# Highs and lows of four heads one above the other in one operand of the spread products

## The reference, cut to what matters

```python
xn  = layernorm(x)                                     # x: 32 batches x 512 tokens x 256
q   = heads(xn @ Wq + bq); k = heads(xn @ Wk + bk)     # 16 heads of 16 columns
val = heads(xn @ Wv + bv)
pos = heads(sinusoid @ Wp + bp)
content   = einsum('bhsp,bhtp->bhst', q + u, k)
pos_score = relative_shift(einsum('bhsp,htp->bhst', q + v, pos))
weights   = softmax((content + pos_score) / 4)
att = (weights @ val) @ Wo + bo
out = x + att + routed_ffn(xn)                         # 8 experts, top 128 of 512 tokens, gelu
```

## Time and profile before

| | us |
|---|---|
| median of 3 runs | 5023.73 |
| lowest, highest | 5016.13, 5023.78 |
| the profiled execution | 5030.14 |
| its span in the trace | 5028.3 |

### The profile page before, as it was taken

How to read it: one execution, slowest core, us unless ns; L and a number is a source line. 1 busy time by engine, 2 the same in 40 slices (tenths; PEclk the granted TensorE clock), 3 DMA queues, 4 the chain that set the end, 5 groups by cost and what they waited for, 6 DMA issues and landing times. The chain is left out here.

```text
span 5028.3 us, 126515 instructions
## 1 busy us (share of the span) xinstructions
PE 4825.9 (96%) x42412; PEld 3683.7 (73%) x42412; DVE 3691.6 (73%) x8040; ACT 3462.9 (69%) x5180; POOL 1711.7 (34%) x1545
## 2 busy tenths in 40 slices
PE   7899999999999999999999999989999999999997
PEld 3566666676676666766666667758999898998997
DVE  7799998898898888988888889874455545444344
ACT  3688888898888888988978889864433333344454
POOL 1122222232223222322222222224566565544443
PEclk9899999999999999999999999999999999999999
DMA  9899999999999999999999999986445455433359
GB/s 351 318 361 347 332 360 342 351 361 337 366 349 345 362 335 346 366 343 359 359 328 360 339 344 366 366 296 179 100 115 141 113 133 140 109 62 68 60 146 312
DMA packets 320461, 1391.16 MB, mean 277 GB/s; under 512 B 42912, under 2 KB 120608, under 8 KB 188448
## 3 DMA queue, kind: packets, MB, share of 16 engines
q1 hardware_dynamic: 196896, 778.35, 41.7%
q0 software_dynamic: 122880, 604.05, 39.3%
HBM read 708.00 MB, written 674.23 MB: 275 GB/s over the span
## 5 line engine op out<-in xcount | busy, mean ns | idle before, releaser
L745 DVE CUSTOM_DVE_ANT_0 att_shifted<-att_quad,att_shifted 128x512 f32<-128x512 f32 x2048 | 1327.1, 684 | 213.2 <-PE att_quad L990 170.5
L610 ACT ACTIVATE att_shifted<-att_shifted,att_mn 128x512 f32<-128x512 f32 x2048 | 1361.9, 717 | 122.0 <-issue 100.4
L605 ACT ACTIVATE ring<-att_quad 128x1024 f32<-128x1024 f32 x1024 | 1047.1, 1023 | 310.8 <-PE att_quad L978 309.5
L1011 PE MATMUL att_tp<-ident,att_shifted 128*128 128x128 f32 x8192 | 1134.4, 282 | 7.1 <-issue 4.4
L755 DVE COPY att_pt<-att_tp 128x512 f32<-128x512 f32 x1536 | 1011.8, 686 | 141.2 <-PE att_tp L1011 124.0
L1011 PEld LDWEIGHTS att_tp<-ident,att_shifted 128*128 128x128 f32 x8192 | 886.8, 142 | 308.3 <-issue 145.4
L497 POOL DMA_DIRECT2D att_shifted<-xs_d x512 | 279.3, 545 | 2249.7 <-DMA xs_d<-ring 1259.3
L1482 DVE TENSOR_TENSOR ffn_hp<-ring,ffn_hp 128x512 fp32r<-128x512 f32 x512 | 474.6, 927 | 683.8 <-ACT ring L1419 638.3
L1417 ACT ACTIVATE ffn_hp<-ffn_up 128x512 fp32r<-128x512 f32 x512 | 306.0, 598 | 920.5 <-PE ffn_up L1563 864.8
L978 PE MATMUL att_quad<-att_pos,att_qv 64*128 64x512 f32 x2048 | 848.1, 454 | 38.3 <-ACT ring L605 38.2
L990 PE MATMUL att_quad<-att_kd,att_qu 64*128 64x512 f32 x2048 | 787.0, 456 | 68.9 <-issue 50.0
(11 more groups left out here) (111 smaller groups left out, 4707.7 us busy)
## 6 DMA issues: line engine op xcount, KB each, us to landing
xs_d<-ring SPq DMA_DIRECT2D x512, 1026.0 KB, 9.4
att_shifted<-xs_d POOLq DMA_DIRECT2D x512, 1024.0 KB, 9.9
att_shifted<-in_L_attn_x_dram SPq DMA_DIRECT2D x32, 512.0 KB, 7.2
xn_d<-att_shifted SPq DMA_DIRECT2D x32, 512.0 KB, 6.5
xt_d<-att_shifted SPq DMA_DIRECT2D x32, 512.0 KB, 7.6
gathered<-xt_d SPq DMA_DIRECT2D x32, 512.0 KB, 11.6
att_d<-att_osb SPq DMA_DIRECT2D x512, 32.0 KB
ring<-in_L_ffn_w_dram SPq DMA_DIRECT2D x16, 1024.0 KB
```

The source lines that it names most:

```text
L605: act.activation(xo[:, kk % NW, 2 * half:2 * half + 2, 1:S + 1], xp[:, :, :], ACT.Copy).then_inc(x_out, 1)
L610: act.activation(shifted[:, kk % NX, t], shifted[:, kk % NX, t], ACT.Exp, bias=mn[:, kk % NX, t:t + 1], scale=-1.0).then_inc(exp_done, 1)
L745: dve.tensor_tensor_reduce(out=shifted[:, kk % NX, t], in0=sp_[:, t % 2], in1=shifted[:, kk % NX, t], scale=-0.25, scalar=-NEG, op0=ALU.ad ...
L1011: ins = pe.transpose(tp[:, c % 2, t * P:(t + 1) * P], shifted[:, kk % NX, t, c * P:(c + 1) * P], ident[:, :])
```

## The change

Four heads (64 rows) are taken at a time. The high parts of four heads stand in one half of the partitions and their low parts in the other half of the same operand, so that `spread_out` is one product where it was two. `qc[:, k, 0]` held the highs of a tile's eight heads and `qc[:, k, 1]` their lows. Now index 0 holds the highs of the first four heads (partitions 0 to 63, `FORMER`) above the lows of the same four (64 to 127, `LATER`), and index 1 the same of the last four. `kc` likewise.

For that POOL's split of a tile, a copy and a subtraction over 128 partitions, becomes four instructions, each behind the one before: the copy of all highs; the subtraction for the last four heads, within their half; the subtraction for the first four, which reads partitions 0 to 63 and writes 64 to 127; and a copy of the last four's highs, which reads 64 to 127 and writes 0 to 63. The last three have 64 partitions and the same 512 elements in each. The counts of the semaphores `high` become three a tile. At the start, ACT and DVE split the two tiles of positions in the same manner (one more instruction each a tile). The constant `spread` is loaded whole in one DMA, where a cleared tile and eight small loads were. The scores, softmax, values and the FFN phase are untouched.

```diff
     spread = np.zeros((P, 2, 2, P), np.float32)
-    for head in range(MH):
+    for head in range(QH):
         for kind in range(2):
             for copy in range(COPIES):
-                row = head % GH * ROWS + copy * HD
-                spread[head * HD:(head + 1) * HD, kind, 1 - picks_high[kind][copy], row:row + HD] = np.eye(HD)
+                column = head % GH * ROWS + copy * HD
+                row = head * HD if picks_high[kind][copy] else P // 2 + head * HD
+                spread[row:row + HD, kind, head // GH, column:column + HD] = np.eye(HD)
...
-                sp.wait_ge(spread_zero, 1)
-                for kind in range(2):
-                    for k in range(MH // GH):
-                        rows = slice(k * GH * HD, (k + 1) * GH * HD)
-                        at = spread_at[kind] + k * P
-                        sp.dma_start(spread[rows, at:at + P].bitcast(F32), spread_d[rows, kind, 0]).then_inc(const_in, 16)
+                sp.dma_start(spread[:, :, :, :].bitcast(F32), spread_d).then_inc(const_in, 16)
...
                     pool.tensor_copy(by_tile(qc[:, k, 0]), in_order(qn[:, k])).then_inc(high, 1)
-                    wait_alone(pool, high, v + 1)
-                    pool.tensor_tensor(by_tile(qc[:, k, 1]), in_order(qn[:, k]), by_tile(qc[:, k, 0].bitcast(F32)),
+                    wait_alone(pool, high, v * 3 + 1)
+                    pool.tensor_tensor(by_tile(qc[LATER, k, 1]), in_order(qn[LATER, k]), by_tile(qc[LATER, k, 0].bitcast(F32)),
+                                       ALU.subtract).then_inc(high, 1)
+                    wait_alone(pool, high, v * 3 + 2)
+                    pool.tensor_tensor(by_tile(qc[LATER, k, 0]), in_order(qn[FORMER, k]), by_tile(qc[FORMER, k, 0].bitcast(F32)),
                                        ALU.subtract).then_inc(low, 1)
+                    wait_alone(pool, low, v + 1)
+                    pool.tensor_copy(by_tile(qc[FORMER, k, 1]), in_order(qn[LATER, k])).then_inc(high, 1)
+                    wait_alone(pool, high, v * 3 + 3)
...
                     act.wait_ge(q_full, v + 1)
+                    wait(act, qu_high, v * 3)
                     wait(act, qu_low, v)
+                    wait(act, qv_high, v * 3)
                     wait(act, qv_low, v)
+                    wait(act, k_high, v * 3)
                     wait(act, k_low, v)
...
-                def spread_out(bank, kind, g, high, low):
-                    at = spread_at[kind] + g % (MH // GH) * P
-                    pe.matmul(bank, spread[:, at:at + P], high, start=True, stop=False)
-                    at = at - spread_back[kind]
-                    return pe.matmul(bank, spread[:, at:at + P], low, start=False, stop=True)
+                def spread_out(bank, kind, g, stacked):
+
+                    half = g % (MH // GH) // (QH // GH)
+                    return pe.matmul(bank, spread[:, kind, g % (QH // GH), :], stacked[:, half], start=True, stop=True)
...
                     v = i * TILES + g // (MH // GH)
-                    pe.wait_ge(qu_high, v + 1)
                     pe.wait_ge(qu_low, v + 1)
-                    spread_out(mp[:, :], QUERIES, g, qc[:, 0, 0], qc[:, 0, 1]).then_inc(qu_full, 1)
+                    pe.wait_ge(qu_high, v * 3 + 3)
+                    spread_out(mp[:, :], QUERIES, g, qc[:, 0]).then_inc(qu_full, 1)
```

More of the change, by code:

```diff
@@ L38 @@
 NEG = -3.0e38
+FORMER = slice(0, P // 2)
+LATER = slice(P // 2, P)
 SPLITS = ((0, 0), (0, 1), (1, 0))
@@ L168, in attention_phase @@
         xg = shared.tokens()
-        spread_at = (QH // GH * HD, QH // GH * HD + MH // GH * P + HD)
-        spread_back = (QH // GH * HD, HD)
-        spread = m.sb("spread", [P, spread_at[1] + MH // GH * P], F32R)
+        spread = m.sb("spread", [P, 2, QH // GH, P], F32R)
         vectors = m.sb("vectors", [P, 5, DC])
@@ L231, in attention_phase @@
         padded = m.sem("padded")
-        spread_zero = m.sem("spread_zero")
         eps_set = m.sem("eps_set")
@@ L409, in store_o @@
                                      osb[row:row + 1, q % 2]).then_inc(o_stored[q % 2], 16)
-                sp.wait_ge(p_low, DC)
+                sp.wait_ge(p_low, DC * 2)
                 sp.wait_ge(w_low, 1)
@@ L441, in _ @@
             def _(pool):
-                pool.memset(spread[:, :].bitcast(F32), 0.0).then_inc(spread_zero, 1)
                 pool.memset(val[:, :, :, :, :], 0.0).then_inc(ones_set, 1)
@@ L477, in keys @@
                     pool.tensor_copy(kc[:, 0], qn_k).then_inc(k_high, 1)
-                    wait_alone(pool, k_high, v + 1)
-                    pool.tensor_tensor(kc[:, 1], qn_k, kc[:, 0].bitcast(F32), ALU.subtract).then_inc(k_low, 1)
+                    wait_alone(pool, k_high, v * 3 + 1)
+                    pool.tensor_tensor(kc[LATER, 1], qn_k[LATER], kc[LATER, 0].bitcast(F32), ALU.subtract).then_inc(k_high, 1)
+                    wait_alone(pool, k_high, v * 3 + 2)
+                    pool.tensor_tensor(kc[LATER, 0], qn_k[FORMER], kc[FORMER, 0].bitcast(F32), ALU.subtract).then_inc(k_low, 1)
+                    wait_alone(pool, k_low, v + 1)
+                    pool.tensor_copy(kc[FORMER, 1], qn_k[LATER]).then_inc(k_high, 1)
+                    wait_alone(pool, k_high, v * 3 + 3)
                 def split_xt(b, s):
@@ L504, in _ @@
                 with_u(0, 0)
-                pool.wait_ge(p_low, DC)
+                pool.wait_ge(p_low, DC * 2)
                 pool.wait_ge(w_low, 1)
@@ L559, in keep_positions @@
                     act.activation(qc[:, c, 0], (mp, op)[c][:, :], ACT.Identity, bias=bias_p[:, c:c + 1]).then_inc(p_high, 1)
+                    act.activation(qc[FORMER, c, 1], (mp, op)[c][LATER, :], ACT.Identity, bias=bias_p[LATER, c:c + 1]).then_inc(p_high, 1)
                 def keep_queries(i, t):
@@ L701, in position_lows @@
                 def position_lows(c):
-                    dve.wait_ge(p_high, c + 1)
-                    dve.scalar_tensor_tensor(qc[:, c, 1], (mp, op)[c][:, :], bias_p[:, c:c + 1], qc[:, c, 0].bitcast(F32), ALU.add,
+                    dve.wait_ge(p_high, c * 2 + 1)
+                    dve.scalar_tensor_tensor(qc[LATER, c, 1], (mp, op)[c][LATER, :], bias_p[LATER, c:c + 1], qc[LATER, c, 0].bitcast(F32), ALU.add,
+                                             ALU.subtract).then_inc(p_low, 1)
+                    dve.wait_ge(p_low, c * 2 + 1)
+                    dve.scalar_tensor_tensor(qc[LATER, c, 0], (mp, op)[c][FORMER, :], bias_p[FORMER, c:c + 1], qc[FORMER, c, 0].bitcast(F32), ALU.add,
                                              ALU.subtract).then_inc(p_low, 1)
@@ L1040, in _ @@
                     if 6 <= b < 6 + NG8 // 2:
-                        pe.wait_ge(p_low, DC)
+                        pe.wait_ge(p_low, DC * 2)
+                        pe.wait_ge(p_high, DC * 2)
                         spread_positions(2 * (b - 6))
```

13 lines of the change are left out of this document (7 added, 6 removed).

## The result

The changed kernel takes 5206.7 us (median of 4 runs, 5196.6 to 5214.8); the kernel before took 5023.8 us beside it. The ratio is 1.0375, with a 95% interval from 1.0354 to 1.0396. Forecast were 5010 us, with a range up to 5075. The profiled execution took 5214.75 us, its span is 5213.0.

What follows compares the result with a forecast made beforehand. PE's order of work sets the pace today; after the change, transfers bound between stops. Terms -36 + 12 + 12 - 2 = -14 us, from 5023.7 us, gave 5010 us, with a range of 4945 to 5075.

Steps and rivals of the forecast that it cites:

- What bounds the kernel before: In attention, PE's order of work sets the pace, with the DMA engines full between stops at iteration starts.
- The second product, 0.32 us of PE, 3.84 in eight heads: In each spread, the removed product frees 0.32 us of PE, 3.84 us per eight heads, 248 us in all.
- POOL's splits at full price, `with_u` 5.8 us: On POOL, 64-partition instructions cost as much as 128-partition ones, so with_u goes from 2.85 to 5.8 us.
- L578 waits, PE stands 2 us, up to 3: At kk % 8 = 6, ACT's query copy waits for with_u, and PE stands 2 to 3 us before the key's spread.
- The sum of PE, 46.7 us: PE's time per eight heads between stops: 47.5 - 3.84 + 3.0 = 46.7 us, below the packets' 48.
- a rival of 0.30: At the key's spread, PE's gap halves the clock, costing 2.5 us more per eight heads: 5062 us, chance 0.30.
- Between stops the transfers bound: Between iteration starts, transfers bound and DVE waits for reads; +0.3 us in each of 39 stretches, +12 us.
- After a stop -2.8 us each, -36: After an iteration's start, PE's 3.84 us less 1.0 of POOL's gap count: -2.8 us x 13 = -36 us.
- Iterations 0 to 2, +12: In iterations 0 to 2 DVE is full, removed products give nothing; 1 us in each of 12 tiles, +12 us.
- The start, -2: At the start, one load replaces eight, against one more ACT and DVE instruction per position tile: -2 us.
- Transfers yield: Between stops, transfers can go faster than today, so PE's 46.7 us sets the stretches: 4944 us, chance 0.17.
- POOL's price was neither cheap nor dear: POOL's half-height splits at half price: 4974 us, chance 0.05; at twice the price: 5180 us, chance 0.03.

Runs made afterwards that it cites:

- qn_double: The changed kernel with a second buffer for the queries with u, so ACT's copies need not wait for with_u: 5017.0 us, ratio 0.9958.
- after_light: The changed kernel with reads of the shifted scores a quarter shorter after the first iteration: 5116.3 us, ratio 1.0159.
- high_only: The kernel before with only the product of the highs in each spread, POOL's splits and the start unchanged: 5024.8 us, ratio 0.9966.
- qn_light: The changed kernel with a second buffer for the queries with u and reads a quarter shorter after the first iteration: 4910.8 us, ratio 0.9773.
- pool4_two: The kernel before, both products kept, with POOL's splits of queries and keys in four instructions, none writing across halves: 5232.7 us, ratio 1.0399.

## Why the prediction was wrong

*What bounds the kernel before.* Right. PE's order of work at 47.1 us in eight heads and the DMA engines at about 47.4 stand side by side, as I read them from the earlier trace rows; the lighter reads separate them.

*The second product, 0.32 us of PE, 3.84 in eight heads.* Too large. The distance of two starts in the earlier trace rows was taken for what goes when one of them goes; the spread that is left holds PE for 0.41 us. In eight heads 2.3 us are saved where DVE has less to copy, and 1.6 with DVE full in the odd heads.

*POOL's splits at full price, `with_u` 5.8 us.* Right: from L451's start at 1535.86 to L459's end at 1541.53 are 5.7 us. So was the rule of the Trainium skill (GPSIMD Engine Reference, "Elementwise — side-by-side cycle accounting") that I had set beside it: half the partitions cost the same 1.55 us.

*L578 waits, PE stands 2 us, up to 3.* Right in place and, at 3.0 us on average, at my upper value.

*The sum of PE, 46.7 us.* **This is the step that failed.** It put PE below the transfers' 48 us, and two of its terms were wrong by about as much: the removed products at 3.84 us, where 1.6 arrive, and the granted clock's fall behind a stop of 3 us at nothing, with a rival of 0.30 for it. It fell in 53 of 56 tiles, 2.1 us each. From what was measured the sum is 47.1 - 1.6 + 3.0 + 2.1 = 50.6 us; the stretches took 51.2 on average (50.9, 51.3 and 51.5). The two heads behind a stop are slower even without a fall, 11.98 us less their idle time against 11.59 in `qn_double` (46 tiles), which is most of what is missing. The term of the clock was priced well there (2.5 us), as were place and mechanism. But the rival's sum, 49.2, had the 3.84 in it, and so it gave 5062 us where 5207 came out; the range ended at 5075 for that reason.

*Between stops the transfers bound.* Wrong for the changed kernel: DVE's wait for reads was to go above 80 us and fell to 2.4. The transfers bear on it in another way, by how late `with_u` can start (`after_light`). Without POOL's stop the statement holds: in `high_only` and `qn_double` the stretches lie at 47.9 and 47.4 us on average, with waits of 54 to 58 us. The forecast described these two kernels, but for the size of the waits.

*After a stop -2.8 us each, -36.* Wrong: these eight heads took 57.7 us against 56.4, and in `qn_double`, without POOL's stop, 56.6; with lighter reads 54.4 (`qn_light`) against 54.9. PE's saving does not shorten the stretch in which an iteration begins.

*Iterations 0 to 2, +12.* The sign was right. It is +34 us: in the tiles of iterations 1 and 2 PE stands 1.1 to 5.1 us, and the clock falls in each. With lighter reads these iterations take 604.2 us against 592.1, so 12 of the 34 us are left, and the rest comes with the transfers.

*The start, -2.* The eight loads became one, of 0.65 us in place of 3.99. But the first add came at 184.3 us against 180.6. Over all traces, it came between 178 and 184 us in the seven kernels with the old start and between 184 and 194 in the seven with the new one: some 5 us later by the mean, not 2 earlier, though the two groups meet at 184. Why was not tried.

*The rivals.* "Transfers yield": in `qn_double` single stretches did come down to 45.5 us, but their mean stayed at 47.4, so it holds for a few and not for the sum. The 425 GB/s that the Trainium skill gives for one core (HBM Reference, "Specifications (TRN2)") are not reached over eight heads: 377 in the window shown, at a share of 1.01, and 385 at most in a stretch of `qn_double`. POOL's price was neither cheap nor dear.

## What to carry to other kernels

Before an engine is given more work, follow its slack to the next engine and on to TensorE: here 2.95 us more on an engine that was busy for a third of the time stopped PE for 3 us in each tile. A stop of PE of 2 to 3 us has two prices, the idle time and the slower products behind it, and a forecast should carry both as its main case; shorter stops had both in a part of the cases. If the one instruction that waits overwrites a buffer, a second buffer can be the remedy, as here; the one reordering of PE that was tried did not help, since the wait stands in another engine's queue. And what a removed product saves is the old distance of its neighbours less the new one, bounded by the next full engine.

## What was not expected of the hardware

- The clock after a stop of one length is not one number. In `pool4_two` stops of 2.35, 2.56 and 2.38 us led to a granted clock of 0.81, 1.00 and 0.90 over two heads. In this kernel's stretch from 500 to 3250 us, PE stops of 1.5 to 2 us were followed by half clock in 3 of 11 cases (in a fourth 5.8 us later), of 2 to 3 us in 22 of 25, of 3 to 3.5 us in 17 of 17. In the changed kernel's first two iterations it fell behind stops of 1.1 to 1.3 us too, in four tiles. What decides in the shorter ones stays open.
- A fall costs 2.1 to 2.2 us a tile on average, beside a stop of 2.7 to 3.0 us.
- POOL's instructions on 64 partitions take as long as on 128 (1550 and 1553 ns; 1280 and 1283), whether they write into their own half or the other.
- The DMA engines at a share of 1.00 to 1.01 held the mean stretch of `high_only` and `qn_double` at 47.9 and 47.4 us, though PE and DVE go on at 45.5 with lighter reads. The share does not tell the pace: at 1.01 single stretches of `qn_double` took 45.5 us with 380 GB/s and others 50.4 us with 348 GB/s.
